# Third layer of a transformer kernel: three fp32 products replaced by products of high and low parts

## The reference

```python
xn = (x - mu) * jax.lax.rsqrt(var + EPS) * norm_gamma + norm_beta
shifted = jnp.roll(xn, (-SHIFT, -SHIFT), (1, 2))
dw = conv(shifted, dw_w, 'SAME', feature_group_count=c) + dw_b      # 7 x 7, depthwise
dw_windows = _win_partition(dw, WS)                                 # windows of 7 x 7
qkv = _win_partition(shifted, WS) @ qkv_w.T + qkv_b
attn = softmax(einsum('bhnd,bhmd->bhnm', q * scale, k) + rpb + mask)   # 6 heads of 16
out = einsum('bhnm,bhmd->bhnd', attn, v).reshape(...) + dw_windows
return shortcut + roll_back(window_reverse(out @ proj_w.T + proj_b))
...
```

## Time and profile before

| | us |
|---|---|
| median of 3 runs | 11909.03 |
| lowest and highest | 11908.05, 11911.75 |
| the profiled execution | 11907.59 |
| its span | 11905.8 |
| PE busy in the span | 11196.1 (94%) |
| ACT busy | 7836.3 (66%) |
| DVE busy | 7361.0 (62%) |
| POOL busy | 4375.4 (37%) |

### The profile page before, as it was taken

One profiled execution on the slowest core, in us unless ns is written; L12 is line 12 of the kernel. 1 busy time (PEld: TensorE's weight loads), 2 busy tenths in 40 slices (PEclk: granted clock), 3 DMA queues, 4 the chain that ended last, 5 costly groups with the idle time before them and its releaser, 6 DMA issues. The chain is left out here.

```text
span 11905.8 us, 393166 instructions
## 1 busy us (share of the span) xinstructions
PE 11196.1 (94%) x157972; PEld 8194.0 (69%) x157972; DVE 7361.0 (62%) x12636; ACT 7836.3 (66%) x13524; POOL 4375.4 (37%) x5892
## 2 busy tenths in 40 slices
PE   6999999899999999998989999998999999999999
PEld 3444444577777777777767676766877778777777
DVE  4444444577777777775456666666666666666665
ACT  4555555477777777775346666765777777777776
POOL 0000000377777777774000000001555555555554
PEclk9999999899999999999989999998999999999999
DMA  1111111122222222223643333332010001010000
GB/s 57 36 40 35 40 40 35 36 52 51 51 51 51 51 51 51 51 51 105 215 122 77 76 78 75 78 76 53 24 24 24 24 24 24 24 25 24 24 24 22
DMA packets 1105618, 617.58 MB, mean 52 GB/s; under 512 B 864651, under 2 KB 1076566, under 8 KB 1099704
## 3 DMA queue, kind: packets, MB, share of 16 engines
q1 hardware_dynamic: 1091496, 553.66, 19.2%
q10 hardware_dynamic: 12288, 38.54, 1.0%
HBM read 308.38 MB, written 282.75 MB: 50 GB/s over the span
## 5 line engine op out<-in xcount | busy, mean ns | idle before, releaser
L1485 POOL TENSOR_TENSOR L_HdL<-L_Hd,L_HdH 128x392 fp32r<-128x392 f32 x1536 | 1572.1, 1024 | 283.9 <-POOL L_HdH L1483 283.2
L1469 POOL TENSOR_TENSOR L_SQ<-L_X 96x392 f32<-96x392 f32 x512 | 429.4, 839 | 2316.0 <-DMA L_X<-after_L 2306.4
L985 PEld LDWEIGHTS banks<-L_ident,L_PR 113*113 113x113 f32 x9216 | 1149.4, 181 | 187.9 <-issue 126.8
L985 PE MATMUL banks<-L_ident,L_PR 113*113 113x113 f32 x9216 | 1204.4, 267 | 1.2 <-DVE L_X L1391 0.7
L1220 ACT COPY L_PT<-banks 113x452 f32<-113x452 f32 x1792 | 886.1, 538 | 414.4 <-PE banks L985 414.1
L1236 ACT ACTIVATE L_PR<-L_SX 113x588 f32<-113x588 f32 x1536 | 1087.5, 708 | 51.5 <-DVE L_SX L1363 10.5
L395 PE MATMUL banks<-scan_XS,scan_W1T 97*96 (+1 forms) x2688 | 1113.2, 553 | 0.0
L1533 POOL COPY L_XN<-L_XR 96x392 f32<-96x392 f32 x256 | 147.6, 577 | 2508.2 <-DMA L_XR<-L_norm 2371.3
L1056 PE MATMUL banks<-L_VB,L_PT 113*49 113x34 f32 x36864 | 1063.9, 213 | 1.4 <-ACT L_PT L1220 1.0
L1483 POOL CAST L_HdH<-L_Hd 128x392 fp32r<-128x392 f32 x1536 | 788.6, 513 | 742.8 <-issue 684.1
L1263 ACT ACT_TABLE_LOAD x512 | 656.9, 1283 | 606.2 <-PE banks L992 606.2
(11 more groups left out here) (233 smaller groups left out, 25901.0 us busy)
## 6 DMA issues: line engine op xcount, KB each, us to landing
L_X<-after_L SPq DMA_DIRECT2D x768, 147.0 KB
after_L<-L_X SPq DMA_DIRECT2D x512, 147.0 KB
conv_T<-L_norm_by_phase SPq DMA_DIRECT2D x96, 512.0 KB, 3.3
L_norm_by_phase<-L_XP SPq DMA_DIRECT2D x512, 84.0 KB, 2.1
scan_XT<-in_x SPq DMA_DIRECT2D x33, 1176.0 KB, 7.0
L_norm<-L_XA SPq DMA_DIRECT2D x256, 147.0 KB, 1.9
L_conv<-conv_D ACTq DMA_DIRECT2D x96, 392.0 KB, 3.0
L_XR<-L_norm SPq DMA_DIRECT2D x256, 147.0 KB, 2.4
```

Source lines behind the costliest of these rows:

```text
L985: mm = pe.transpose(bank(TURN[a])[0:SPAN, (k % 4) * SPAN:(k % 4 + 1) * SPAN], PR[:, st.v if lag else st.u, 2 * k:2 * k + 2, :].rearrange(" ...
L1485: pool.tensor_tensor(HdL[:, u, j].bitcast(F32R), Hd[:, u, j], HdH[:, u, j], ALU.subtract).then_inc(s[f"hd_parts_{j}"], 1)
```

## The change

In pass "L2" keys, queries and the product with the convolved rows are computed by parts. split_weights makes high and low parts of Wq, Wk and Wp once. On POOL, to_windows also makes XNH and XNL (a cast and a subtraction), once the queries of two chunks back are done; a new split_convolution makes DWH and DWL from DW, once the projection of two chunks back is done. PE's front waits for xn_parts, project_convolution for dw_parts, and SP's load of DW for dw_parts in place of proj. project stays one fp32 matmul. The reading order of the convolved rows is the same as before.

```diff
@@ sb tiles, set-up @@
+            XNH = sb("XNH", [C + 1, 2, CH]); XNL = sb("XNL", [C + 1, 2, CH])
+            WpH = sb("WpH", [128, C + 1]); WpL = sb("WpL", [128, C + 1])
+            DWH = sb("DWH", [C, 2, PHASES, WS, JW]); DWL = sb("DWL", [C, 2, PHASES, WS, JW])
...
+            split_weights(nc, "L2_parts", [(t[0:C + 1], h[0:C + 1], l[0:C + 1]) for t, h, l in ((Wq, WqH, WqL), (Wk, WkH, WkL), (Wp, WpH, WpL))])
@@ SP @@
                     if kind == "L2":
-                        st.wait("proj", lag + 4)
+                        st.wait("dw_parts", lag + 4)
@@ PE @@
-                def by_parts(out, wh, wl, xh, xl):
+                def by_parts(out, wh, wl, xh, xl, stop=True):
                     for n, (wt, xt) in enumerate(((wh, xh), (wh, xl), (wl, xh))):
-                        mm = pe.matmul(out, wt.bitcast(F32R), xt.bitcast(F32R), start=(n == 0), stop=(n == 2))
+                        mm = pe.matmul(out, wt.bitcast(F32R), xt.bitcast(F32R), start=(n == 0), stop=(n == 2) and stop)
...
                 def keys(st):
-                        pe.matmul(out, Wk[0:C + 1, :], XN[:, st.u], start=True, stop=True).then_inc(s["k"], 1)
+                    by_parts(bank(K_BANK)[0:C, 0:CH], WkH[0:C + 1, :], WkL[0:C + 1, :], XNH[:, st.u], XNL[:, st.u]).then_inc(s["k"], 1)
...
                 def queries(st):
-                        pe.matmul(out, Wq[0:C + 1, :], XN[:, st.u], start=True, stop=True).then_inc(s["q"], 1)
+                    by_parts(bank(Q_BANK)[0:C, 0:CH], WqH[0:C + 1, :], WqL[0:C + 1, :], XNH[:, st.u], XNL[:, st.u]).then_inc(s["q"], 1)
...
                 def project_convolution(st):
-                    st.wait_turn(loaded[st.of4(1)], 1, N_LOADS, 4)
-                    pe.matmul(bank(PROJ_BANK)[0:C + 1, 0:CH], Wp[0:C, :], DW[:, st.of4(1)].rearrange("c p i j -> c i j p"), start=True, stop=False)
+                    st.wait("dw_parts", 1)
+                    raster = lambda t: t[:, st.v].rearrange("c p i j -> c p (i j)").rearrange("c p n -> c n p")
+                    by_parts(bank(PROJ_BANK)[0:C + 1, 0:CH], WpH[0:C, :], WpL[0:C, :], raster(DWH), raster(DWL), False)
...
                 def front(st):
-                    st.wait("xn", 0)
+                    st.wait("xn_parts", 0)
@@ POOL @@
                         pool.tensor_copy(seen(XN[0:C, u]), win(XR[:, u])).then_inc(s["xn"], 1)
+                        st.wait("q", lag + 2)
+                        hold(pool, s["xn"], st.value(lag), passed)
+                        pool.tensor_copy(XNH[:, u].bitcast(F32R), XN[:, u]).then_inc(s["xn_high"], 1)
+                        hold(pool, s["xn_high"], st.value(lag), passed)
+                        pool.tensor_tensor(XNL[:, u].bitcast(F32R), XN[:, u], XNH[:, u], ALU.subtract).then_inc(s["xn_parts"], 1)
+
+                    def split_convolution(st):
+                        st.wait("proj", 2)
+                        hold(pool, loaded[st.of4(0)], (st.t // 4 + 1) * (16 * N_LOADS), passed)
+                        pool.tensor_copy(DWH[:, st.u].bitcast(F32R), DW[:, st.of4(0)]).then_inc(s["dw_high"], 1)
+                        hold(pool, s["dw_high"], st.value(0), passed)
+                        pool.tensor_tensor(DWL[:, st.u].bitcast(F32R), DW[:, st.of4(0)], DWH[:, st.u], ALU.subtract).then_inc(s["dw_parts"], 1)
...
+                        if st.f:
+                            split_convolution(st)
```

## The result

The changed kernel is faster: 11,813.10 us median (11,807.14 to 11,814.36, 4 runs) against 11,910.39 for the kernel before (11,908.05 to 11,922.95, 4 runs), a ratio of 0.9915 with the interval 0.9898 to 0.9932. I had forecast 12,030 us, with 0.10 for "faster". The profiled execution took 11,807.14 us, 100.5 less than before's 11,907.59.

A forecast was written before the change was run, and what follows sets the result against it. Two chains, TensorE's own and VectorE's to O, were taken to bound L2's chunk together. 11907.6 + 118 (product) + 4 (once), with keys, queries and POOL at 0, gave 12029.6, against the median 12,030 us; range 11,950 to 12,245, chance 0.80.

The forecast's parts named there:

- faster: Whole kernel: a gain of more than 0.2% (24 us), the outcome of Rival 3 and Rival 6, chance 0.10.
- Keys and queries counted at 0: Keys and queries in L2: 0.28 us of PE saved per chunk, counted at 0; bounds 0 and 0.03 us.
- O's hold: Heads' transposes in L2: they wait for VectorE's O; in the last chunk PE idles 1.30 us for it.
- The product by parts, 0.46 us more per chunk: Product with the convolved rows in L2: three fp32r passes, 1.29 us instead of 0.83, 118 us in all.
- the surcharge of fp32: Product with the convolved rows: alternating addresses cost each fp32 pass 86 ns more, taken as SBUF's delivery limit, 0.415 us.
- the convolution pass's breaks: Convolution pass: 16 address breaks cost an fp32r pass 21 ns, gone at half clock, so read as a delivery limit.
- Rival 3: Product with the convolved rows: fp32 reads columns more than once, an fp32r pass takes 0.21 us; 11,871 us, chance 0.09.
- What it gains or loses counts whole: Product with the convolved rows: behind O and ahead of the next scores, its change counts fully, 256 times.
- POOL's work at 0: POOL's casts and subtractions in L2: 4.0 us of each 7.9 to 8.3 us chunk, in time, cost 0.
- rival 5: POOL's new work in L2: blocks VectorE's SBUF subtraction ahead of O, likelier some 0.4 us per chunk; 12,130, chance 0.05.
- Once +4 us: Weights' parts and first keys' wait for one cast and one subtraction: some 4 us in all, once.
- Rival 6: Heads' transposes: O doesn't hold them, the 0.28 us of keys and queries counts; 72 us less, chance 0.01.

The follow-up runs named there:

- e1: Kernel before with only keys and queries by parts, the product with the convolved rows left in fp32: 11,854.91 us, ratio 0.9952.
- e3: Changed kernel with the parts of the convolved rows read in the order in which they lie: 11,814.89 us, ratio 0.9919.
- e4: Kernel before with the convolved rows read in fp32 in the order in which they lie: 11,900.76 us, ratio 0.9989.
- e7: Changed kernel with the parts of the convolved rows read four numbers on from column to column: 11,915.23 us.
- e13: Changed kernel with the parts of the convolved rows read two numbers on from column to column: 11,902.31 us.

## Why the prediction was wrong, point by point

**Keys and queries counted at 0: right.** e1 shows a chunk of 7.863 us. In the full change they brought 0.04 us from the keys to the heads' transposes (1.394 to 1.356), about the upper bound given. What I missed is their second use: ScalarE's ring, in which they let the chunk gain 0.187 us with the product where the product alone gains 0.063. The last chunk of "L2" after the change, which has no keys ahead of the heads, shows O's hold unchanged, 1.30 us as in the earlier trace rows:

```profile
8140.52 1.05 PE L991 MATMUL banks<-L_ident,L_PR 113*113 113x113 f32 x8
...
8145.11 0.59 PE L1061 MATMUL banks<-L_ident,L_O 113*96 113x113 f32 x4 [1.30 <-DVE L_O L1379]
```

**The product by parts, 0.46 us more per chunk: this step failed, and the sign with it.** The prediction took the strided fp32 pass (0.415 us) as the time in which SBUF delivers such addresses, and let fp32r meet the same limit. It takes 0.166 us, and the three with the change of type 0.57 instead of the 1.29 forecast. Two inferences broke: first, that the surcharge of fp32 belongs to the address alone; e3 and e4 show that in the same order one type pays 0.17 us for the product and the other nothing; second, that the convolution pass's breaks speak for a delivery limit in this order. That a surcharge which goes away at half clock is a limit and not arithmetic holds for fp32 in this order (e1, e4) and for parts whose columns step on by two or four numbers (e7, e13, 0.35 to 0.38 us). What failed is carrying it over to rounded floats in this order, where there is no surcharge at all. Rival 3 had the right sign: a quarter of the fp32 product, 0.21 us a pass, 0.67 in all (0.57 measured), 11,871 us. It had 0.09. Without the jumps the change would stand near 11,870 us too, but that is luck: its product gains 0.26 us and not 0.16, and OT takes back a part. The rival's reason, that an fp32 matmul reads its columns more than once (four reads for the product, two for each of its two instructions), fits where the rows lie in order (0.662 / 4 = 0.166 us against 0.18 for a pass by parts) and for four numbers on (1.365 / 4 = 0.341 against 0.37). For rows in turn it is too small a part: 0.208 against 0.166 with two rows, 0.330 against 0.21 with four. By these ratios the forecast's mistake was to take the 0.415 us of one fp32 pass for one delivery of its 392 columns; this is argued, since no run shows the reads themselves.

**"What it gains or loses counts whole": right upwards, wrong downwards.** In e7 the product is 0.28 us longer than in before and the chunk 0.23; keys and queries save 0.04 and the heads' transposes 0.03, and small spacings cost 0.02. Downwards the product lost 0.26 and the chunk 0.19, since the projection then waited for OT. The earlier trace rows shows no row of ScalarE. Had I followed OT as I followed O, its small slack would have been seen: in the same chunk of before, ScalarE's copy ends at 7310.96, and the projection's weight load starts 0.10 us later, where it starts 0.05 us behind the copy when TensorE waits for it.

```profile
7310.41 0.55 ACT L1303 COPY L_OT<-banks 96x196 f32<-96x196 f32 x2
7311.06 0.26 PEld L1073 LDWEIGHTS banks<-L_OT,L_Wp 97*97 97x97 f32 x2
```

**POOL's work at 0: right.** It is busy for 3.9 us of a chunk (852.4 us more in the whole, 3.3 for each of 256 chunks), and nothing on TensorE waits for the parts. The blocking that rival 5 feared is there, 1.10 us for the second subtraction instead of 0.77 in the chunk shown and over 0.9 us in a quarter of the chunks, and it falls where the prediction put it, behind O. VectorE's way from the scores to O is unchanged (4.41 us).

**Once +4 us: nearly right.** Up to the first heads' transposes of "L2" it is 2.4 us from the end of the convolution pass on.

**Rival 6 was counted on the wrong side.** 72 us less than the forecast is 11,958 us, slower than before and not faster; so the prediction's own sum for "faster" was 0.09 and not 0.10.

**Missed: the jumps,** some 60 of the 100 us, half of them in a pass that the change doesn't touch. No term of the sum and no rival had the change's effect on where code lies. The stalls were to be seen in before: two put to "issue" at each jump, 5 us and a halved clock behind them, nine times in each of three passes. That the change would take one of them away twice was luck of position.

## What to carry to other kernels

Before pricing a shorter operation, list every chain that passes through the place where it is, on every engine, with its slack: here three lay within 0.06 us of each other (TensorE's own work and O at 7.86, OT at 7.80), and only turning round two orders on ScalarE and VectorE together released 0.38 us a chunk (7.675 to 7.299). Look for idle time put to "issue" behind a long loop's jump, and if code grows or shrinks, expect it to change: compare the jump's chunk apart from the median one. Don't carry a surcharge from one type or one order of addresses to another; measure that pass alone.

## What the runs showed of the hardware that I had not expected

- Rounded floats read alternately from two rows 196 numbers apart cost 0.166 us for 392 columns, less than read in order (0.18); fp32 pays 0.83 against 0.66 us for its product. A step of two or four numbers costs a pass by parts 0.35 to 0.38 us.
- Orders of columns that cost more at full clock cost nothing or little more at half clock: 0.35 us a pass by parts with a step of four numbers at either level (e7), while the alternating order goes from 0.166 to 0.327.
- A jump back over a loop of 24 chunks costs TensorE one stall of some 3 us or two (3 and 2 us), by where the loop lies in the code, and leaves the granted clock at 0.50 for 3 to 10 us. The second ends 1.15 to 1.72 us behind the landing of the next 16.4 KB of code, and is not there when TensorE needs 4 us or more to reach that code. 94 instructions of shift moved an unchanged kernel by 42 us of 11,909.
- Waits that have long been reached are not free: from the first keys of "L2" to its first scores it is 10.25 us with 188 of them and 17.75 us with 324, some 0.055 us each (3.5 and 2.9 us without any). "L2" comes 7.6 and 14.9 us later by them.
